# Token reads of the SyncE queue grouped by batch, and a new order of work on the compute engines, in a four-layer conditional sequence kernel

## The reference

```python
# layer 0: diffusion, with reflected borders
x = x + zX * lap_x(x) + zY * lap_y(x) + zR * x * (1 - x)
# layer 1: additive attention, the mask chosen by token itok_B_0_2 (prefix, postfix, all but own)
scores = tanh(x @ W1 + b1) @ v
p = softmax(where(mask[itok_B_0_2], scores, -1e30))
x = x + (p @ x) / count(mask)
# layer 2: linear layer, weights chosen by token itok_B_0_7 (of 8)
x = x + x @ weight[itok_B_0_7].T + bias[itok_B_0_7]
# layer 3: adapter, profile chosen by token itok_B_0_6 (of 8)
z = relu(x @ down_w[itok_B_0_6] + down_b)
y = x + z @ up_w[itok_B_0_6] + up_b
x = x + layernorm(y) * ln_g + ln_b
```

## Time and profile before

| | us |
|---|---|
| median of 3 runs | 618.41 |
| the profiled execution, its own time | 617.02 |
| its span, first to last instruction | 615.2 |
| TensorE busy in it | 546.9 |
| VectorE busy | 461.7 |
| GpSimd busy | 319.7 |
| ScalarE busy | 312.7 |

### The profile page before, as it was taken

How to read it: one execution, slowest core, us unless ns; L and a number is a source line. 1 busy time by engine, 2 the same in 40 slices (tenths; PEclk the granted TensorE clock), 3 DMA queues, 4 the chain that set the end, 5 groups by cost and what they waited for, 6 DMA issues and landing times.

```text
span 615.2 us, 9135 instructions
## 1 busy us (share of the span) xinstructions
PE 546.9 (89%) x2838; PEld 430.6 (70%) x2838; DVE 461.7 (75%) x1164; ACT 312.7 (51%) x545; POOL 319.7 (52%) x283
## 2 busy tenths in 40 slices
PE   8968799999679995999949999599994999999995
PEld 3557568887378873888639886488864887588774
DVE  7358767998279983699746996579945899688577
ACT  5545653576235861457515585246842557453520
POOL 4175515882277812877119772187623884235431
PEclk9998899999979999799988999799996999999998
DMA  7874392927878369765598556893578926632443
GB/s 244 281 165 108 111 324 48 200 83 191 253 175 173 88 176 302 158 142 108 162 322 147 142 115 198 272 188 105 114 214 249 216 72 144 155 66 55 98 95 99
DMA packets 63941, 100.82 MB, mean 164 GB/s; under 512 B 10893, under 2 KB 16525, under 8 KB 63894
## 3 DMA queue, kind: packets, MB, share of 16 engines
q0 software_dynamic: 16544, 29.90, 29.6%
q1 hardware_dynamic: 38096, 53.54, 26.5%
q10 hardware_dynamic: 9254, 16.81, 7.5%
HBM read 67.43 MB, written 31.98 MB: 162 GB/s over the span
## 4 chain that ended last, share of the span: by engine, by line
PE 48%; DVE 17%; DMA 13%; SPq 9%; issue 6%; POOL 4%; ACT 2%; DVEq 0%; ACTq 0%; POOLq 0%
PE y L689 20%; DMA bd_col<-in_L_cond_down_b 8%; PE front_ps L770 6%; SPq L372 5%; PE front_ps L828 4%; PE front_ps L689 4%; PE front_ps L747 3%; POOL x2l L593 3%; DMA out<-x 3%; DMA out<-o_sb 3%; DVE x2f L1546 2%; DVE o_sb L1578 2%; DVE pn L1500 2%; PE front_ps L703 2%; DVE stats L1562 1%
## 5 line engine op out<-in xcount | busy, mean ns | idle before, releaser
L556 POOL TENSOR_TENSOR xd<-xn 128x1024 f32<-128x1024 f32 x28 | 61.0, 2193 | 83.8 <-ACT xn L1009 78.0
L689 PE MATMUL y<-wth,x2h 128*128 128x512 f32 x256 | 104.0, 406 | 0.0
L582 POOL DMA_DIRECT2D out<-o_sb x58 | 60.3, 1156 | 80.3 <-ACT o_sb L1149 79.3
L689 PE MATMUL y<-wth,x2l 128*128 128x512 f32 x256 | 100.1, 391 | 0.0
L689 PE MATMUL y<-wtl,x2h 128*128 128x512 f32 x256 | 100.0, 391 | 0.0
L593 POOL TENSOR_TENSOR x2l<-x2f,x2h 128x1024 fp32r<-128x1024 f32 x32 | 77.9, 2434 | 41.0 <-ACT x2h L1009 39.2
L575 POOL TENSOR_TENSOR norm<-norm 128x1 f32<-128x1 f32 x64 | 57.7, 904 | 61.1 <-DVE norm L1573 61.1
L1546 DVE SCALAR_TENSOR_TENSOR x2f<-alb,small,front_ps 128x128 f32<-128x128 f32 x256 | 71.1, 339 | 2.5 <-POOL x2l L593 1.3
L828 PEld LDWEIGHTS front_ps<-th_pt,x 128*128 128x128 f32 x512 | 62.4, 193 | 6.6 <-DVE x2f L1546 4.0
L828 PE MATMUL front_ps<-th_pt,x 128*128 128x129 f32 x512 | 65.3, 279 | 1.9 <-DVE x2f L1546 0.6
L1009 ACT ACTIVATE x2h<-x2f 128x1024 fp32r<-128x1024 f32 x32 | 34.0, 1061 | 47.7 <-DVE x2f L1546 47.7
(11 more groups left out here) (138 smaller groups left out, 1165.0 us busy)
## 6 DMA issues: line engine op xcount, KB each, us to landing
xn<-in_x SPq DMA_DIRECT2D x32, 512.0 KB, 8.8
out<-x ACTq DMA_DIRECT2D x58, 256.0 KB, 4.0
out<-o_sb POOLq DMA_DIRECT2D x58, 256.0 KB, 5.8
xu<-in_x SPq DMA_DIRECT2D x21, 512.0 KB, 9.8
xu<-in_x POOLq DMA_DIRECT2D x21, 512.0 KB, 7.5
wn_wd<-in_L_cond_weight SPq DMA_DIRECT2D x8, 1024.0 KB, 5.9
wn_wd<-in_L_cond_down_w SPq DMA_DIRECT2D x8, 256.0 KB, 6.7
up_row<-in_L_cond_up_b SPq DMA_DIRECT2D x8, 256.0 KB, 8.1
```

The lines of the kernel that those rows point to most:

```text
L556: pool.tensor_tensor(xd[:, c % 2, :, :], xn[:, c, :, 0:D], xn[:, c, :, 2:D + 2], ALU.add).then_inc(pool_a, 1)
L582: pool.dma_start(out[bass.ds(b, 1), blk(t), :].rearrange("b p d -> p (b d)"), o_sb[:, t % OB, :], accum_op=ALU.add).then_inc(stored[t % OB ...
L689: ins = mm(dst, lhs, rhs, start=first and q == 0, stop=last and q == len(parts) - 1, skip_group_check=True)
```

## The change

Three things change.

The tokens. A new `load_tokens(n)` reads the three tokens of a batch one after the other and keeps them in registers. `load_rows`, `load_linear`, `load_scale` and `load_mask` take them from there. It is called once for a batch, at the end of SP's list for the batch before; for batch 0 it stands before `load_linear(0)`. A batch's reads fall from six to three.

```diff
+            tokens = {}
+
+            def load_tokens(n):
+                tokens[n] = (token(itok_B_0_7, n, NSUB), token(itok_B_0_6, n, NPROF), token(itok_B_0_2, n, 3))
+
             def load_rows(n):
-                subject = token(itok_B_0_7, n, NSUB)
-                profile = token(itok_B_0_6, n, NPROF)
+                subject, profile, _ = tokens[n]
...
             def load_linear(n):
-                subject = token(itok_B_0_7, n, NSUB)
-                profile = token(itok_B_0_6, n, NPROF)
+                subject, profile, _ = tokens[n]
...
             def load_scale(n):
-                profile = token(itok_B_0_6, n, NPROF)
+                profile = tokens[n][1]
...
             def load_mask(n):
-                kind = token(itok_B_0_2, n, 3)
+                kind = tokens[n][2]
...
                 load_above(1, 1)
+                load_tokens(0)
                 load_linear(0)
...
                 load_scale(0)
+                load_tokens(1)
...
                     load_next(m, 3)
+                    if m + 1 < B:
+                        load_tokens(m + 1)
```

More of the change, by code:

```diff
@@ L611, in first @@
                 start_sum(0)
+                rest_up(0, 0)
                 rest_x2(0, 0, 0)
-                rest_up(0, 0)
                 rest_x2(0, 0, 1)
@@ L620, in steady @@
             def steady(b, n, m, q):
-                rest_difference(n)
                 if m is not None:
                     left_and_right(m, 0)
+                    add_below(m, 0)
+                    add_below(m, 1)
                 root(b, 1)
-                if m is not None:
-                    add_below(m, 0)
-                    add_below(m, 2)
                 finish(b, 0)
-                if m is not None:
-                    add_below(m, 1)
-                    add_below(m, 3)
-                start_sum(n)
-                root(b, 2)
                 if m is not None:
@@ L637, in steady @@
                 rest_up(n, q)
+                root(b, 2)
+                rest_difference(n)
+                if m is not None:
+                    add_below(m, 2)
+                start_sum(n)
+                root(b, 3)
                 finish(b, 1)
                 rest_x2(n, q, 0)
+                if m is not None:
+                    add_below(m, 3)
                 finish(b, 2)
+                root(b, 4)
                 rest_x2(n, q, 1)
-                root(b, 3)
-                root(b, 4)
                 if m is not None:
@@ L1165, in opening @@
                 reflect(0, 0)
+                square(0)
                 scale_edges()
@@ L1255, in steady @@
                     centre(m, 0)
+                seed(b, 5)
                 round_x2(n, q, 1)
-                store_base(b, 4)
                 seed(b, 6)
+                scale(b, 2)
                 scale(b, 3)
-                seed(b, 7)
                 if m is not None:
                     scale_rows(m, 1)
-                scale(b, 4)
-                round_x2(n, q, 2)
-                store_base(b, 5)
+                store_base(b, 4)
                 if m is not None:
                     scale_rows(m, 2)
+                scale(b, 4)
+                seed(b, 7)
+                store_base(b, 5)
+                round_x2(n, q, 2)
+                if m is not None:
+                    scale_rows(m, 3)
                 round_x2(n, q, 3)
@@ L1275, in steady @@
                 adapter_relu(n, 0)
+                if m is not None:
+                    reflect(m, 3)
                 adapter_relu(n, 1)
@@ L1675, in steady @@
                 maxima(n)
+                moments(b, 1)
+                block_weights(n)
+                subtract_mean(b, 1 - q, 1)
                 keep_x3(b, 2)
-                block_weights(n)
-                moments(b, 1)
-                subtract_mean(b, 1 - q, 1)
                 row_weights(n)
```

150 lines of the change are left out of this document (73 added, 77 removed).

## The result

| | before | after |
|---|---|---|
| median of the runs, us | 618.22 (617.59 to 618.74, 4 runs) | 558.22 (555.42 to 560.55, 4 runs) |
| the profiled execution's own time | 617.02 | 555.42 |
| its span | 615.2 | 553.6 |
| mean granted clock | 0.950 | 0.992 |

The ratio is 0.9028 (95% interval 0.8983 to 0.9073). The forecast was 570 us with a range from 561 to 584. The changed kernel is faster by 12 us more than forecast, and outside the range.

The account below looks back on a forecast made before the run. The prediction took TensorE's waits for late weights, held behind SP's token reads, as the bound, with the clock second. 617.0 - 37.6 - 12.1 - 1.2 + 2.7 = 568.8 us, given as 570 us for the median, range 561 to 584.

Parts of the forecast that it names:

- What binds, and the token reads: TensorE waits for late weights; three token reads on SP's path go, so the weights start about 7.2 us earlier.
- The waits, 37.6 us saved: TensorE's wait in front of the block sums falls from 44.5 to 6.9 us.
- the unchanged journey: The weights travel as long as before, so they land 7.2 us earlier, at 309.2; the ends were 305.7 and 313.2.
- The lost rest, 2.7 us charged: Periods starting without TensorE's long wait run 1.1 us longer; half was charged for five periods, 2.7 us lost.
- the neighbours that change places in `steady`: Reordered calls in the steady part, costed at nothing each, between minus and plus 1 us a period.
- The clock, 12.1 us saved: The 10 us windows behind TensorE's five long waits lose 12.1 us to throttling; all of it comes back.
- The rule on half of the throttled time: Skill rule pricing the whole kernel's clock loss at 31 us; not used, all regained it would give 551 us.
- `rest_up` in `first`, 1.2 us: In `first`, moving `rest_up` ahead of the rests of x2 takes it out of the chain: 1.2 us saved.
- (b): Rival: weights early and orders bring more, journey 7.8 us, wait zero, small bubbles gone; 561 to 564 us, chance 0.14.
- (c): Rival: TensorE finds new bubbles of 2 to 3 us a period all over; 582 to 588 us, chance 0.10.
- (a): Rival: weights late behind x, 4 us added to each journey, clock may keep dropping; 590 to 602 us, chance 0.09.
- (d): Rival: slower, POOL becomes the bound; at 9 to 10 us a period on the path 626 us, chance 0.02.

Follow-up runs that it names:

- e1: Kernel before with only the token reads grouped one batch ahead, all compute engines in their old order: 573.41 us.
- e9: Kernel before with the load of the next weights moved ahead of the wait for `g_row`, all token reads kept in place: 561.99 us.
- e2: Kernel after with the token reads back in their old places, so the new orders alone: 611.26 us.
- e5: Kernel after with `load_mask` reading its own token again, one read between chunk 0 of x and the weights: 582.91 us.
- e10: e1 with one POOL call, `rest_difference(n)`, moved behind `root(b, 2)`: 566.76 us.
- e16: e9 with one POOL call more moved, `start_sum(n)` behind `root(b, 2)`: 557.21 us.
- e3: Kernel before with eight idle matmuls on TensorE ahead of the block sums in the five periods with a long wait: 618.12 us.
- e8: e2 with seven idle matmuls on TensorE ahead of the block sums in the five periods with a long wait: 606.88 us.
- e4: Kernel after with the weights' load moved ahead of x and the mask, right behind `g_row`: 557.14 us.
- e13: Separate kernel running rows of VectorE and POOL operations alone and together: 16 two-tile VectorE sums took 16.1 us beside POOL, 9.7 undisturbed.

## Why the prediction was right and wrong

- **What binds, and the token reads.** Right. The wait for weights held the path, the weights start 7.0 us earlier against `g_row` (7.2 forecast), TensorE's long waits go, and the clock behind L790 is 1.00. e1 shows the tokens' part alone: 45 us. e9 shows what the prediction did not ask: the reads cost that much only because the weights stood behind the wait for `g_row`. One of its side sums is off: reads at the floor would have saved 3.6 us less in each of five periods, which is 18 us and not "some 15".
- **The waits, 37.6 us saved.** Mis-sized: all 44.5 went, 6.9 us more. The step that failed is "I take 309.2, the unchanged journey". The way from the weights' issue to `add_identity` was 9.0 us on average and not 11.3. Two windows of 2 us, from 4 us behind their issue, first of before (DMA share and GB/s at the row's end), then of after:

```profile
309.10:311.10 2.00, 1.00 1.11 247
311.10:313.10 2.00, 1.00 0.95 206
```

```profile
274.35:276.35 2.00, 2.00 (x15) 1.76 (x13) 0.38 (x2) 1.85 (x3) 0.00 (x0) 1.00 1.01 379
276.35:278.35 2.00, 2.00 (x7) 0.90 (x6) 1.42 (x5) 2.00 (x5) 1.09 (x2) 1.00 1.13 305
```

  At a DMA share of 1.0 or more, 4 to 6 us behind the issue, 379 GB/s moved instead of 247. Before, two stores of POOL (305.42 and 306.57) and one of ScalarE (307.27) were issued among the weights; after, the stores come at 275.46 and 277.76, more than 5 us behind the weights' issue. I had named both directions and let them cancel. The first window moved 200 to 261 GB/s in all five long periods before, and 350 to 379 after. In e1, with the old orders, it moved 346 to 394, the way is 9.1 us, and in the batch of the table POOL's two stores come 7.3 us behind the weights' issue; in e2, with the new orders, they come 0.4 us behind it and the way is 10.4. So the shorter way belongs to the earlier start and not to the new orders. That the stores are the cause is read from these traces and was not isolated; what is left of x counts in the GB/s as well. With 2.3 us less, `add_identity` is at 12.7 us behind `g_row`; adding the 6.2 us of the shortest way gives 18.9, and TensorE comes to the block sums at 63.7 - 44.0 = 19.7. So the wait is zero, by 0.8 us on average and by 0.0 to 1.5 in the single periods. With the 15 us forecast it would have been 1.5. The result hung on that margin, which e5 shows from the other side.
- **The lost rest, 2.7 us charged.** Wrong for the change, right for a part. The periods that start without rest take 63.7 us, as those behind a long wait did with their clock loss taken off. In e1 the bubbles come as feared, larger even: 15 us in all. They are not a lack of rest but, as far as was tested, operations of VectorE stretched by POOL, hidden before by TensorE's wait: e10 shows it for 7 of the 15 us, and e16 against e9 shows 5 us for the probabilities, of which TensorE's waits in front of L802 show 2.7 (8.2 to 5.5). The step that failed is costing "the neighbours that change places in `steady`" at nothing. The earlier trace rows had the sign of it, POOL's sum of 1.26 us that takes 4.4, and I used it only for the rival in which POOL is the bound.
- **The clock, 12.1 us saved.** The clock came back as said; the size can't be separated. In the order of before, e3 gave back two thirds of the missing clock and no time, so there the windows' loss was not on the path as I took it to be: `g_row`'s release had another chain of equal length. With the tokens and new orders that chain is shorter (44.0 us to `g_row`, against 46.5), 2.5 us in each of five periods, which is the size of the clock term; e8 against e2 puts 1.7 of them beside the clock, but by traces alone. The rule on half of the throttled time (the Trainium skill, TensorE: Matmul & The Clock Gate, HAM oscillation) would have given the whole 31 us; e3 shows that no such sum is right where the matmuls are not what ends last.
- **`rest_up` in `first`, 1.2 us.** The opening gave 2.8 us in the profiled execution. The first block sums come 1 to 2 us earlier or later between kernels whose opening is the same (95.85 after, 97.78 in e4), so this neither confirms nor refutes it.
- **The rivals.** What came is nearest to (b), "the weights are early and the orders bring more", with 0.14: journey shorter, wait zero, bubbles gone. Its lowest number was 561, since it left out what the opening and the end gave (2.6 us more than forecast). (c), new bubbles, is e1 without the orders: 573. (a) fell: x ahead of the weights cost TensorE nothing, as e4, which takes it away, shows, though `add_identity` then starts 10.9 us behind `g_row` instead of 12.6. (d) fell: POOL is not the bound, but it works through VectorE.

The sum with what was measured: 61.6 us gained in the profiled executions and 48.2 forecast (37.6 + 12.1 + 1.2 - 2.7). Of the 13.4 us missing, 6.9 are waits, 2.7 the bubbles that did not come, 2.6 lie outside the six periods (3.8 gained against 1.2), and 1.2 us is rest that no run settles. Between the medians the forecast was 11.8 us too slow; the profiled execution of the kernel after is the fastest of its four.

## What to carry to other kernels

When a queue issues its transfers in program order, look first at what a late transfer stands behind and whether it needs to: here it was a wait for another tile's release and reads of other transfers' addresses, and moving one call (e9) gave 56 us without touching either. When you take a long wait away, read again the operations it hid: VectorE's operations on two SBUF tiles lose most of the time in which POOL's sums run beside them (6.2 of 7.6 us and 6.4 of 10.0 in e13), and the remedy is to move one of the pair to where VectorE reads PSUM or has slack, one call at a time, with the trace in hand. A predicted wait of zero needs its margin written beside it, for 3.5 us over a margin of 0.8 cost 25 us in eight batches.

## What the runs showed of the hardware

- VectorE and POOL block each other in SBUF operations. Undisturbed, VectorE's two-tile sum of 128x512 takes 0.68 us and POOL's 1.26. Beside each other, single ones took up to 3.48 us on VectorE (e1) and 4.46 us on POOL (`start_row`). While POOL ran, 128x128 operations of VectorE lost 6.2 of 7.6 us (e13).
- Who gives way depends on the pairing: in e13 POOL's sums went from 1.27 to 1.30 us at their median beside the 128x128 form, and to 1.71 beside the 128x512 form; in e1 POOL's one sum took 4.44 us beside eight of the 128x128 form. Why is open.
- Keeping TensorE's clock up by idle work (e3, 0.950 to 0.982 on average) gave no time where another chain set the moment of release.
